# The opening of a fused attention and expert kernel, rebuilt over VectorE, ScalarE, GpSimd and two DMA queues, and its maxima run 14 units ahead instead of 16

## The reference, cut to what matters

```python
x = x + layernorm(attention(layernorm(x)))
x = x + layernorm(ffn(layernorm(x)))

# attention, per batch b and head h
q = (x @ q_w.T + q_b) / sqrt(dh); k = x @ k_w.T + k_b; v = x @ v_w.T + v_b
attn = softmax(q @ k.T); out = (attn @ v) @ out_w.T + out_b

# ffn: top 8 of 16 experts by sigmoid(l2norm(x) @ l2norm(gate_w).T), weights normed over the 8
routed = sum_e combine[e] * (silu(x @ w_gate[e]) * (x @ w_up[e])) @ w_down[e]
shared = silu(x @ sw_gate) * (x @ sw_up) @ sw_down
```

## Time and profile before

| what | value |
|---|---|
| median of 3 runs | 2874.84 us |
| lowest and highest | 2865.7 and 2875.46 us |
| the profiled execution's own time | 2873.4 us |
| its span in the profile | 2871.6 us |
| busy share of the span | TensorE 96%, VectorE 78%, ScalarE 57%, GpSimd 33% |
| first score matmul of batch 0 | at 101.32 us |
| granted TensorE clock, mean | 0.985 of full speed |

### The profile page before, as it was taken

The page is one execution under the profiler, slowest core; times in us unless marked ns, Lnnn a source line. Parts: engine busy times, 40 slices in busy tenths (PEclk is TensorE's granted clock), DMA queues, the critical chain, the costliest instruction groups (busy, mean ns, idle before and its releaser), DMA issues.

```text
span 2871.6 us, 47584 instructions
## 1 busy us (share of the span) xinstructions
PE 2760.4 (96%) x16514; PEld 1690.1 (59%) x16514; DVE 2241.4 (78%) x4679; ACT 1634.0 (57%) x3095; POOL 954.1 (33%) x997
## 2 busy tenths in 40 slices
PE   4999999999999999999998899999999999999997
PEld 2434333443343333433433378888888888888886
DVE  4898999999999989999999657666666666666664
ACT  1477777777777777777777743333333333333332
POOL 4041462543534634535335455111111111111112
PEclk8799999999999999999999999999999999999999
DMA  5213323343143234332332233222222222323221
GB/s 91 51 27 57 64 61 56 60 83 59 50 64 64 48 56 64 75 59 48 64 64 75 80 78 95 74 80 82 82 78 81 72 78 82 82 78 80 80 71 55
DMA packets 136639, 197.32 MB, mean 69 GB/s; under 512 B 22336, under 2 KB 84816, under 8 KB 134352
## 3 DMA queue, kind: packets, MB, share of 16 engines
q1 hardware_dynamic: 136400, 194.29, 30.7%
HBM read 108.74 MB, written 17.30 MB: 44 GB/s over the span
## 4 chain that ended last, share of the span: by engine, by line
PE 81%; DVE 6%; SPq 6%; ACT 3%; issue 2%; POOL 1%; DMA 1%; POOLq 0%; ACTq 0%; DVEq 0%
PE o_bank L544 14%; PE y_bank L667 13%; PE g_bank L653 13%; PE u_bank L653 13%; PE sm_bank L534 12%; PE st_bank L522 7%; DVE score_max L1017 4%; SPq L331 4%; PE job_bank L568 3%; ACT probs L906 2%; PE job_bank L577 2%; PE job_bank L589 1%; SPq L344 1%; SPq L356 1%; PE job_bank L608 1%
## 5 line engine op out<-in xcount | busy, mean ns | idle before, releaser
L1017 DVE TENSOR_REDUCE score_max<-sm_bank 128x1 f32<-128x512 f32 x2048 | 1300.8, 680 | 118.3 <-PE sm_bank L534 114.8
L906 ACT ACTIVATE probs<-st_bank 128x512 f32<-128x512 f32 x2048 | 1090.0, 600 | 340.3 <-PE st_bank L522 337.9
L534 PE MATMUL sm_bank<-qk_stack 64*128 64x512 f32 x2048 | 806.9, 466 | 28.0 <-DVE score_max L1017 14.0
L522 PE MATMUL st_bank<-qk_stack 64*128 64x512 f32 x2048 | 764.6, 456 | 31.0 <-ACT probs L906 26.9
L534 PEld LDWEIGHTS sm_bank<-qk_stack 64*128 64x128 f32 x2048 | 333.8, 188 | 594.9 <-DVE score_max L1017 548.8
L544 PE MATMUL o_bank<-probs,v_quad 128*32 128x512 f32 x4096 | 550.7, 610 | 6.5 <-ACT o_sb L814 6.5
L1174 DVE TENSOR_TENSOR h<-gate_act,u_bank 128x512 f32<-128x512 f32 x256 | 176.2, 688 | 314.4 <-ACT gate_act L868 314.4
L868 ACT ACTIVATE gate_act<-g_bank 128x512 f32<-128x512 f32 x272 | 162.4, 597 | 416.0 <-PE u_bank L653 415.9
L522 PEld LDWEIGHTS st_bank<-qk_stack 64*128 64x128 f32 x2048 | 318.7, 185 | 112.6 <-ACT probs L906 84.7
L879 ACT ACTIVATE h_hi<-h 128x512 fp32r<-128x512 f32 x272 | 172.1, 633 | 327.7 <-DVE h L1177 290.0
L667 PE MATMUL y_bank<-f_w_hi,h_hi 128*128 128x256 f32 x1088 | 311.8, 287 | 0.1
(11 more groups left out here) (197 smaller groups left out, 3857.5 us busy)
## 6 DMA issues: line engine op xcount, KB each, us to landing
cb<-comb_dram SPq DMA_DIRECT2D x256, 256.0 KB, 3.6
qk_stack<-qk_parts SPq DMA_DIRECT2D x360, 128.0 KB
x_in<-in_x SPq DMA_DIRECT2D x8, 1024.0 KB, 6.8
o_part<-o_sb SPq DMA_DIRECT2D x256, 32.0 KB, 2.0
sum_part<-o_sb SPq DMA_DIRECT2D x256, 32.0 KB, 2.0
x_res<-in_x SPq DMA_DIRECT2D x16, 512.0 KB, 3.9
x<-x_res SPq DMA_DIRECT2D x16, 512.0 KB, 3.1
f_x_in<-x SPq DMA_DIRECT2D x16, 512.0 KB, 3.9
```

The lines of the kernel that those rows point to most:

```text
L522: mm(st_bank[tile % RING][:, :], k_stack[q][p][rows, kc * CH:(kc + 1) * CH], q_stack[q][p][rows, f * HALF:(f + 1) * HALF], start=True, sto ...
L534: mm(sm_bank[n % RING][:, :], q_stack[q][p][rows, tok:tok + CH], k_stack[q][p][rows, half * HALF:(half + 1) * HALF], start=True, stop=True ...
L906: nc.scalar.activation(probs[kc % 2][:, j, :], st_bank[(4 * U + j) % RING][:, :], ACT.Exp).then_inc(exp_done, 1)
L1017: v.reduce_max(score_max[f][:, HC * (2 * p + e) + c, half:half + 1], sm_bank[n % RING][:, :], AX_X).then_inc(smax_read, 1)
```

## The change

It has five parts.

1. **Layer norm and weights.** VectorE now takes all of the first layer norm: the root (12 small operations in a chain, `first_rstd`) and the norm itself (8 operations of 128x256). ScalarE makes the high parts of the weights, VectorE the low parts of q and k, GpSimd those of v and o, between `set_stacks(0)` and `set_stacks(1)`. The bias and identity loads go out from ScalarE's queue.
2. **Four banks.** The first `XT`, `QK` and `V` jobs use `job_bank`, `o_bank` and two banks of the score ring in turn.
3. **Stacks of batch 0 from two queues.** SP issues the six DMAs of a quad's first pair, ScalarE those of its second (`load_pair`). ScalarE's six of quad 0 stand before the reading of `QK` job 4, its eighteen others after that of job 7 and before that of the `V` jobs. The two small zeroing DMAs are dropped for batch 0, since the stacks have been set to zero already. `load_x(1)` and `load_shift(0, 0)` now come after the last stack.
4. **V jobs among the first maxima.** Half a `V` job follows each of the first eight groups of four maxima.
5. **LOOK = 14.** The maxima run 14 units ahead: 56 are done in the opening and the last end two units later. `combine_maxima` and the `SH` jobs move from units 8s and 8s + 1 to unit 8s + 2, and `shift_row` from 8s + 2 to 8s + 3. Some small steps of the expert stage's first group move by one unit (51 for 50 and so on).

```diff
+LOOK = 14
-    JOBS[8 * _s + 1] = ("SH", 0, _s + 1, None)
+    JOBS[8 * _s + 16 - LOOK] = ("SH", 0, _s + 1, None)
-        first_bank = [job_bank, o_bank]
+        first_bank = [job_bank, o_bank, st_bank[0], st_bank[1]]
...
+        def load_pair(engine, B, q, p):
+            m = q // 2
+            for j in (2 * p, 2 * p + 1):
+                h, base = 4 * q + j, 64 * (j % 2)
+                src = slice(DH * (h % 8), DH * (h % 8) + DH)
+                for rows, pair in ((0, slice(0, 4, 2)), (16, slice(1, 3)), (48, slice(0, 4, 3))):
+                    engine.dma_start(qk_stack[q][base + rows:base + rows + DH, p, :, :].bitcast(F32),
+                                     projected(B, m)[src, pair, :].bitcast(F32)).then_inc(stack_loaded[q], 16)
...
             for q in range(QUADS):
-                if q == QUADS - 1:
-                    load_x(1)
-                    load_shift(0, 0)
                 sp.wait_ge(stacks_set, 5 * (q + 1))
-                load_stack(0, q, True)
+                sp.wait_ge(job_read["QK"], nth("QK", 0, 4 * (q // 2) + 3))
+                load_pair(sp, 0, q, 0)
+                sp.sem_inc(stack_loaded[q], 32)
+            load_x(1)
+            load_shift(0, 0)
...
-            for S in range(2):
-                for n in range(4 * CHUNKS):
-                    smax(S, S, n // 4, n // 2 % 2, n % 2)
-                if S == 0:
-                    job("SH", 0, 0)
-            for i in range(4):
-                job("V", 0, i, job_bank=first_bank[(i + 1) % 2], banks=2)
+            for M in range(LOOK):
+                for n in range(4):
+                    smax(M // CHUNKS, M // CHUNKS, M % CHUNKS, n // 2, n % 2)
+                if M < CHUNKS:
+                    job("V", 0, M // 2, M % 2, job_bank=first_bank[M // 2], banks=4)
+                if M == CHUNKS:
+                    job("SH", 0, 0, job_bank=first_bank[0], banks=4)
+            pe.wait_ge(job_read["V"], nth("V", 0, 3))
...
+            for n in "qkvo":
+                act.wait_ge(w_raw_loaded[n], 16)
+                nc.scalar.activation(w_parts[n][0][:, :, :], w_raw[n], ACT.Copy,
+                                     scale=DH ** -0.5 if n == "q" else 1.0).then_inc(weights_hi, 1)
...
             for n, (kind, i) in enumerate(FIRST_JOBS):
-                job(kind, 0, i, first_bank[n % 2])
+                if (kind, i) == ("QK", 4):
+                    load_other_pair(0)
...
+                job(kind, 0, i, first_bank[n % 4])
+            for q in range(1, QUADS):
+                load_other_pair(q)
             for i in range(4):
-                job("V", 0, i, first_bank[(i + 1) % 2])
+                job("V", 0, i, first_bank[i])
...
+            first_rstd()
+            for c in range(CHUNKS):
+                v.tensor_scalar(x_in[:, c, :], x_in[:, c, :], mv_x[:, c, 0:1], rstd_x[:, c:c + 1],
+                                ALU.subtract, ALU.mult).then_inc(x_normed, 1)
...
-                    if kc == 0 and not (last and s == STEPS - 1):
+                    if kc == 16 - LOOK and not (last and s == STEPS - 1):
                         combine_maxima(S + 1, (s + 1) % 2)
```

More of the change, by code:

```diff
@@ L187, in both_stages @@
         bias_set = sem("bias_set")
-        weights_split = sem("weights_split")
+        w_raw_loaded = {n: sem(f"w_raw_loaded_{n}") for n in "qkvo"}
+        bias_loaded = sem("bias_loaded")
+        weights_hi = sem("weights_hi")
+        weights_lo = {"dve": sem("weights_lo_dve"), "pool": sem("weights_lo_pool")}
+        first_chain = sem("first_chain")
         x_loaded = sem("x_loaded")
@@ L317, in load_x, with load_stack @@
                 sp.dma_start(x_in[:, :, :], xv[:, bass.ds(B * CHUNKS, CHUNKS), :]).then_inc(x_loaded, 16)
-            def load_stack(B, q, first):
-                m = q // 2
-                sp.wait_ge(job_read["QK"], nth("QK", B, 4 * m + 3))
-                if not first:
-                    sp.wait_ge(st_ready, 4 * (UNITS * (B - 1) + 16 * (q + 1)))
-                for j in range(4):
-                    h, p, base = 4 * q + j, j // 2, 64 * (j % 2)
-                    src = slice(DH * (h % 8), DH * (h % 8) + DH)
-                    for rows, pair in ((0, slice(0, 4, 2)), (16, slice(1, 3)), (48, slice(0, 4, 3))):
-                        sp.dma_start(qk_stack[q][base + rows:base + rows + DH, p, :, :].bitcast(F32),
-                                     projected(B, m)[src, pair, :].bitcast(F32)).then_inc(stack_loaded[q], 16)
+            def load_stack(B, q):
+                sp.wait_ge(job_read["QK"], nth("QK", B, 4 * (q // 2) + 3))
+                sp.wait_ge(st_ready, 4 * (UNITS * (B - 1) + 16 * (q + 1)))
+                for p in range(2):
+                    load_pair(sp, B, q, p)
                 for base in (0, 64):
@@ L700, in batch @@
                     U, S = UNITS * b + u, STEPS * b + s
-                    maxima = s + 2 < STEPS or not last
+                    M = U + LOOK
+                    maxima = M < UNITS * BATCHES
+                    if maxima and M % (2 * CHUNKS) == 0:
+                        pe.wait_ge(stack_loaded[M // (2 * CHUNKS) % QUADS], STACK_INC * (M // UNITS + 1))
                     if kc == 0 and s % 2 == 0:
-                        if maxima:
-                            B2 = b if s < 6 else b + 1
-                            pe.wait_ge(stack_loaded[(s // 2 + 1) % QUADS], STACK_INC * (B2 + 1))
                         pe.wait_ge(v_copied, QUADS * b + s // 2 + 1)
@@ L1281, in batch @@
                     s, kc = u // CHUNKS, u % CHUNKS
-                    S = STEPS * b + s
-                    maxima = s + 2 < STEPS or not last
-                    if kc == 0 and not (last and s == STEPS - 1):
+                    U, S = UNITS * b + u, STEPS * b + s
+                    M = U + LOOK
+                    maxima = M < UNITS * BATCHES
+                    if kc == 16 - LOOK and not (last and s == STEPS - 1):
                         combine_maxima(S + 1, (s + 1) % 2)
@@ L1469, in _, with first_weight_lo @@
             wait_apart(pool, two_set, 1, passed["pool"])
+            def first_weight_lo(n):
+                wait_apart(pool, weights_hi, "qkvo".index(n) + 1, passed["pool"])
+                g.tensor_tensor(w_parts[n][1][:, :, :], w_raw[n], w_parts[n][0][:, :, :].bitcast(F32),
+                                ALU.subtract).then_inc(weights_lo["pool"], 1)
             set_stacks(0)
-            norm_x(0)
+            for n in "vo":
+                first_weight_lo(n)
             for q in range(1, QUADS):
```

126 lines of the change are left out of this document (72 added, 54 removed).

## The result

The changed kernel takes 2918.1 us (median of 4 runs, 2906.4 to 2921.0), the kernel before 2872.2 us beside it: a ratio of 1.0157, with a 95% interval of 1.0131 to 1.0182. It is slower by 46 us (45.1 between the two profiled executions), where 2876 was forecast and 2890 was the upper end of the range. The profiled execution took 2918.49 us with a span of 2916.7, against 2873.4 and 2871.6.

A forecast was written before the change was run, and what follows sets the result against it. It took TensorE and VectorE to go in step in the batches, after an opening that is a chain. From 2873.4: less 25.0 (opening), plus 19.6 (waits), 7.0 (clock) and 1.0 (end) gave 2876.0 us, range 2850 to 2890.

The forecast's parts named there:

- the opening: Everything up to the first scores: they come at 76.3 instead of 101.32, giving back 25.0 us (bounds 17 and 33).
- seven waits for shift rows, and the clock behind them: Batches 1 to 7: TensorE stands 2.8 us longer in each, 19.6 us, plus 7.0 us for the lowered clock.
- the end (steps 59 to 64): End of the kernel: two more units carry maxima at a low clock, costing 1.0 us (5 gained to 3 lost).
- I take 0.3: Opening: VectorE norms one 128x256 chunk in 0.3 us, so all of x is normed at 15.7.
- GpSimd's part costs nothing: Opening: GpSimd's low parts and fifteen settings end near 27, long before the stacks of quads 1 to 3 are copied.
- the truth is nearer to the upper end: 11.8: Opening: from SP's first stack DMA to the first maximum takes 11.8 us, between 7.2 and 14.4.
- I take 2.7: Opening: each of eight groups of four maxima with half a `V` job takes 2.7 us, between 2.4 and 3.8.
- one set of DMA engines: Rival, chance 0.23: in the opening all stack copies go at today's rate; scores start at 84.1, time 2883.8.
- I add 1.0 us for each: Batches 1 to 7: slow clock after each of seven stalls costs 1.0 us, 7.0 in all (bounds 0 and 10).
- the clock stays low after each stall: Rival, chance 0.12: at unit 15 of seven batches each stall costs 4.9 us in place of 1.0, giving 2903.
- The shift load isn't late after all: Rival, chance 0.20: something in the batches takes up the 2.8 us, giving 2849.4.
- scores after 84: Sign of error in the opening: if scores start above 84, a wait there is missing from the forecast.

The follow-up runs named there:

- the new opening alone: The change with the maxima 16 units ahead as before, shift job and first expert steps moved back: 2873.0 us, ratio 1.0005 to the kernel before.

## Why the prediction was wrong

It forecast 2876.0 and a range up to 2890; it was 2918.5 in the profiled execution. The waits of the batches came in the place and for the cause that it named, but too small in its sum; the opening and the end were wrong in their steps too, and the steps between were put at nothing. By its terms:

| term | forecast, us | measured, us |
|---|---|---|
| the opening | -25.0 | -5.9 (step 1), -7.1 (first scores) |
| seven waits for shift rows, and the clock behind them | +26.6 | +37.3 (32.6 in batches 1 to 6, 4.7 in step 58) |
| the other steps | 0 | +3.9 |
| the end (steps 59 to 64) | +1.0 | +9.8 |

**The opening, 19 us of the error.** First scores were forecast at 76.3 and came at 94.27, 18.0 us later. *"I take 0.3"* for a normed chunk was right for the instruction and wrong for its place: with GpSimd at work beside it a chunk takes 0.93. Together with the way to the stacks, that made SyncE start 4.7 us late (31.92 for 27.2). Of these, 4.2 are the norm, which ended at 19.9 where 15.7 was forecast, and 0.6 the way from there. *"GpSimd's part costs nothing"* is the step that failed: it cost the 4.8 us by which the norm is longer, since GpSimd's work, though it ends in time for the stacks, slows VectorE's while it runs. *"the truth is nearer to the upper end: 11.8"*: the first maximum came 17.5 us after the first DMA, beyond my upper bound of 14.4. With one queue it is 15.6, so 1.9 us are quad 1's copies that the second queue lets in between, and 3.8 are my hope for a rate that the engines don't have; together 5.7 us. *"I take 2.7"* for a group with half a `V` job: 3.87, the 3.8 of my upper bound, as the clock stayed at 0.50 throughout; the way from the first maximum to the `SH` job took 33.3 us in place of 24.0, 9.3 more. From the `SH` job on it took 11.6 us rather than 13.3, since ScalarE had begun to read the `V` jobs when TensorE came (79.47, against 82.7). The sum is 4.7 + 5.7 + 9.3 - 1.7 = 18.0. The rival "one set of DMA engines" was right in its mechanism, 48 DMAs at no more than the old rate; its 84.1 for first scores was still 10 us early, for the two other reasons.

**The waits, right in place and cause.** All seven came at the unit named, behind the queue named. Putting that load ahead of one quad's stacks removed every one. In size: the load for step 1 was late by 2.6, as forecast, but SyncE took 1.2 us longer from there to the load for step 2, so the added wait was 3.6 us and not 2.8 (in batches 1 to 6 TensorE's waits are 23.2 us after, 1.9 before). I had held the length of the chain fixed and given the term a bound of 21 us that nothing in the trace supported; the seven waits added 24.6.

**The clock behind a wait was under-priced.** *"I add 1.0 us for each"*. Five of the kernels, the change and those with 14 ahead in which the load was left where it was, have 30 such waits in their batches 1 to 6. They are 1.74 to 5.20 us long, 106.9 us in all, and the two steps around them lose 162.3 us against before. Before has 1.9 us of such waits in the same places, so the five kernels added 97.5, and 64.8 us are left: 2.2 us for each wait beyond what was added to it (1.6 to 2.8 by kernel). In the change itself the seven waits are longer by 3.5 us each and cost 5.3: a price of 1.8. The stall of the earlier trace rows was followed by a unit of 3.75 us; here one of 5.74 follows a longer one. Waits longer than forecast by 0.7 and a price higher by 0.8, seven times, are the 10.7 us by which this term was short. That the price is the clock's rests on the rows at 0.50 behind the waits and on their absence before; no run changed the clock alone.

**The end was missed.** The late chain on SyncE's queue reaches one thing more than shift loads: the weights in the last batch. The working followed the queue as far as *"the gather, and the load for step 2"* and stopped there. The third step of the last batch loses 7.9 of the 9.8 us. When only the queue's order was mended, 3.6 of these remained, and with the weights ahead 0.4: 3.2 us belong to the weights, and 4.3 to the late chain in another way. In that step fall the end of the low clock behind the shift wait, TensorE's wait of 3.08 us and a clock of 0.57 behind it (1566 to 1570); how the 4.3 divide between them is not shown.

**The steps between were put at nothing.** They lose 3.9 us, and the same steps lose 3.2 to 4.3 in every kernel with 14 units ahead: the nearer maxima cost this by themselves, for a reason that no run shows.

Of the rivals, "the clock stays low after each stall" named the right side and came to 2903, but by luck: its 4.9 us for each stall is far above the 1.8 measured, and it too gave the opening 25.0. "The shift load isn't late after all" fell. What the forecast said would show it wrong, scores after 84, is what the profile shows.

## What to carry to other kernels

Moving one small job by one unit costs what the queue behind it makes of it: follow the queue to its last consumer, and look first for bulk transfers with slack standing ahead of a small urgent one, since swapping the two was worth 46 us here (2918.1 to 2872.2) and brought no new wait in batches 1 to 6. A second issuing engine does not bring a second set of DMA engines: what it overtakes is later by it. And before work is added to an idle engine, see what the other engines are doing at that moment, since they can slow it without a wait to be seen, and whether TensorE has a wait of its own, such as the one for the first stack, in which the work is free.

## What the runs showed of the hardware

VectorE's norm of a 128x256 chunk takes 0.33 us alone and up to 1.40 while GpSimd sets memory or subtracts weights; GpSimd's settings take 1.09 us in place of 0.95 in that time. Neither engine shows it as a wait: it lies in the durations.

A wait of 3.6 us of TensorE costs 5.4 against before, which has 0.3 us in the same place (means of 30 in five kernels): behind it the granted clock is at 0.50, 1.2 GHz. The same work of four maxima for each group, on the other hand, loses nothing at that clock, because VectorE's reading, 2.4 us, covers it.

Runs of the same kernel differ with the mean granted clock: among 20 of the kernel before, 2867.1 us had 0.988 and 2878.0 had 0.983. A gain of 2 to 5 us, that the marks of the one profiled execution show up to step 57, can vanish in the medians, as it did with the new opening alone. The marks say where an execution gained or lost; whether a kernel is faster is said by the medians, and here only for differences larger than these.
